# A tap sum and one convolution tap moved between engines in four units of a Hyena-style block (one core)

## The reference, cut to what matters

```
xn    = layernorm(x)
z     = rmsnorm(xn, pre_norm_w) @ in_proj_w.T            # 768 channels
z_pre = causal depthwise conv of z, 3 taps, + short_b
x2, x1, v = split(z_pre)                                 # 256 channels each
h     = sum over 16 states of residues * exp(log_poles * t)
xv    = x1 * v
y     = (longconv(xv, h) + xv * D_skip) * x2
...   # out projection, gated MLP, layernorm, residual, then a second FFN with layernorm
```

## Time and profile before

| | |
|---|---|
| three runs | 1079.39, 1080.0, 1081.58 us; median 1080.0 |
| profiled execution | 1079.64 us, span 1077.8 us |
| busy over the span | PE 98%, DVE 82%, ACT 66%, POOL 28% |
| phase A | to about 189 us of the span |
| phase B | to about 250 us |

### The profile page before, as it was taken

How to read it: one execution, slowest core, us unless ns; L and a number is a source line. 1 busy time by engine, 2 the same in 40 slices (tenths; PEclk the granted TensorE clock), 3 DMA queues, 4 the chain that set the end, 5 groups by cost and what they waited for, 6 DMA issues and landing times.

```text
span 1077.8 us, 24963 instructions
## 1 busy us (share of the span) xinstructions
PE 1054.1 (98%) x9012; PEld 1008.1 (94%) x9012; DVE 880.8 (82%) x2321; ACT 710.9 (66%) x1589; POOL 299.3 (28%) x575
## 2 busy tenths in 40 slices
PE   8899999999999999999999999999999999999998
PEld 7777788889989999999999999989999999999997
DVE  7999998784788788888888778897878888887876
ACT  7878887774465666666666666666656666666644
POOL 6677775460111111211111111121111111111111
PEclk9999999999999999999999999999999999999999
DMA  3337987976533333333333333443333333333000
GB/s 129 119 124 234 296 216 193 378 293 125 108 59 50 50 54 57 50 51 52 55 59 63 60 50 54 119 102 43 53 58 50 51 53 54 58 64 58 22 21 31
DMA packets 112491, 102.83 MB, mean 95 GB/s; under 512 B 7552, under 2 KB 103744, under 8 KB 112112
## 3 DMA queue, kind: packets, MB, share of 16 engines
q1 hardware_dynamic: 111136, 98.67, 41.7%
q0 software_dynamic: 736, 2.51, 0.7%
q10 hardware_dynamic: 496, 0.05, 0.0%
HBM read 75.75 MB, written 30.70 MB: 99 GB/s over the span
## 4 chain that ended last, share of the span: by engine, by line
PE 67%; DVE 7%; issue 2%; ACT 1%; POOL 0%; POOLq 0%; DVEq 0%; ACTq 0%
PE ps_ring L1539 35%; PE ps_w L1539 15%; PE ps_m L1539 9%; PE ps_o L1539 4%; PE ps_rt L1554 2%; DVE base L1361 1%; PE ps_w L1549 1%; DVE bn L1265 1%; PE ps_m L1605 1%; DVE ht_l L1277 1%; DVE prod L1308 0%; DVE pt_l L1277 0%; POOL sc L1117 0%; ACT rows L1242 0%; ACT hid L1203 0%
## 5 line engine op out<-in xcount | busy, mean ns | idle before, releaser
L1117 POOL TENSOR_TENSOR sc<-sc,neg_half 128x2 f32<-128x2 f32 x127 | 94.8, 746 | 677.1 <-DVE sc L1489 405.9
L1182 ACT ACTIVATE gate<-ps_ring 128x256 f32<-128x256 f32 x192 | 72.9, 381 | 125.9 <-PE ps_ring L1539 124.8
L1203 ACT ACTIVATE hid<-ps_ring,b1s 128x256 f32<-128x256 f32 x256 | 112.1, 483 | 27.6 <-PE ps_w L1539 13.3
L1539 PE MATMUL ps_ring<-mt_l,wl_h 128*128 128x256 f32 x640 | 125.8, 278 | 2.6 <-DVE mt_l L1277 2.6
L1539 PE MATMUL ps_ring<-mt_h,wl_h 128*128 128x256 f32 x640 | 125.8, 278 | 1.8 <-DVE prod L1308 1.3
L1539 PE MATMUL ps_ring<-mt_h,wl_l 128*128 128x256 f32 x640 | 125.3, 277 | 0.0
L1277 DVE TENSOR_TENSOR ht_l<-hid,ht_h 128x256 fp32r<-128x256 f32 x256 | 103.2, 423 | 16.6 <-ACT ht_h L1207 10.7
L1539 PE MATMUL ps_ring<-xt_h,we_h 128*128 128x256 f32 x512 | 103.5, 283 | 2.5 <-DVE prod L1308 2.4
L1308 DVE TENSOR_TENSOR prod<-ps_ring,gate 128x256 f32<-128x256 f32 x192 | 80.8, 421 | 24.7 <-ACT gate L1182 21.0
L1539 PE MATMUL ps_ring<-xt_h,we_l 128*128 128x256 f32 x512 | 100.3, 277 | 0.0
L1539 PE MATMUL ps_ring<-xt_l,we_h 128*128 128x256 f32 x512 | 100.3, 277 | 0.0
(11 more groups left out here) (203 smaller groups left out, 2737.1 us busy)
## 6 DMA issues: line engine op xcount, KB each, us to landing
toep_scratch<-taps_scratch SPq DMA_DIRECT2D x26, 512.0 KB, 7.4
toep<-toep_scratch SPq DMA_DIRECT2D x26, 512.0 KB, 7.1
xa<-in_x SPq DMA_DIRECT2D x16, 512.0 KB, 5.1
x_scratch<-x2c SPq DMA_DIRECT2D x16, 512.0 KB, 3.7
x2s<-x_scratch SPq DMA_DIRECT2D x32, 256.0 KB, 6.9
xa_c<-in_x SPq DMA_DIRECT2D x32, 256.0 KB, 2.6
xb_c<-in_x SPq DMA_DIRECT2D x32, 256.0 KB, 2.7
yin<-seq SPq DMA_DIRECT2D x124, 64.0 KB, 6.4
```

Of the source, the lines that this page charges most:

```text
L1117: nc.gpsimd.tensor_tensor(sc[:, to], sc[:, to], neg_half[:, 0, 0:CC], ALU.pow).then_inc(S[done], 1)
L1182: nc.scalar.activation(gate[rows_of, m % 2], ring[m % RING][rows_of, 0], ACT.Gelu_apprx_tanh).then_inc(S["gate_done"], 1)
L1203: nc.scalar.activation(hid[:, m % HIDS], block_of, ACT.Gelu, bias=b1s[:, m:m + 1]).then_inc(S["hid_done"], 1)
L1539: mm = nc.tensor.matmul(out, lhs(a, kk), rhs(b, kk), start=(j == 0), stop=(closed and j == len(todo) - 1))
```

## The change

In the first four units (`u <= LAST_POWERS`, which is 3):

- the sixth block's last tap is made by ScalarE into a second half of `x2_tap` and added by GpSimd, as the fifth's already is, and VectorE's third tap of that block is gone;
- VectorE's second pair of tap sums, which stood behind the fourth block, stands behind the sixth.

In all units `x2_tap` has two halves, and the ring `pole_pow` has 12 tiles in place of 16, which leaves the memory taken as it was. The waits on `x2_done` and `tap_extra` count two additions for each of these units. From unit 4 on the order of the work is the old one.

```diff
-    POWERS = 16
+    POWERS = 12
...
-        x2_tap = sb(ctx, "x2_tap", [P, TA])
+        x2_tap = sb(ctx, "x2_tap", [P, KB, TA])
...
+        def beside(u):
+            return (4, 5) if u <= LAST_POWERS else (4,)
+        def beside_until(u):
+            return sum(len(beside(n)) for n in range(u))
...
-                sp.wait_ge(S["x2_done"], u + 1)
+                sp.wait_ge(S["x2_done"], beside_until(u + 1))
...
-                    pool.wait_ge(S["conv_done"], ZB * n + 5)
-                    pool.wait_ge(S["tap_extra"], n + 1)
-                    nc.gpsimd.tensor_tensor(sums_of(0, n, 2), sums_of(0, n, 2), x2_tap[:], ALU.add
-                                            ).then_inc(S["x2_done"], 1)
+                    for k, i in enumerate(beside(n)):
+                        pool.wait_ge(S["conv_done"], ZB * n + i + 1)
+                        pool.wait_ge(S["tap_extra"], beside_until(n) + k + 1)
+                        nc.gpsimd.tensor_tensor(sums_of(k, n, 2), sums_of(k, n, 2), x2_tap[:, k], ALU.add
+                                                ).then_inc(S["x2_done"], 1)
...
-                if i == 4:
-                    wait(act, S["x2_done"], u)
-                    nc.scalar.activation(x2_tap[:], slot(b)[:], ACT.Copy, scale=sw[:, m, 2:3]
+                if i in beside(u):
+                    wait(act, S["x2_done"], beside_until(u))
+                    nc.scalar.activation(x2_tap[:, m], slot(b)[:], ACT.Copy, scale=sw[:, m, 2:3]
...
-                        if i == 4:
-                            dve.wait_ge(S["tap_extra"], n + 1)
-                        add_tap(n, i, 1, "conv_done" if i == 4 else "mid_done")
+                        if i in beside(n):
+                            dve.wait_ge(S["tap_extra"], beside_until(n) + i - 3)
+                        add_tap(n, i, 1, "conv_done" if i in beside(n) else "mid_done")
...
-                    if valid(n, UA) and i != 4:
+                    if valid(n, UA) and i not in beside(n):
...
-                    if i in (0, 3):
+                    if i in (0, ZB - 1):
                         long_taps(powers_at(n, i))
```

More of the change, by code:

```diff
@@ L358, in carry_x2 @@
             def carry_x2(u):
-                pool.wait_ge(S["x2_done"], u + 1)
+                pool.wait_ge(S["x2_done"], beside_until(u + 1))
                 pool.wait_ge(S["conv_done"], ZB * (u + 1))
@@ L545, in _ @@
                         measure(n + 3, i // 2 if i < 3 else i - 2)
-                    if valid(n, UA) and i != 4:
-                        dve.wait_ge(S["mid_done"], (ZB - 1) * n + (i if i < 4 else 4) + 1)
+                    if valid(n, UA) and i not in beside(n):
+                        dve.wait_ge(S["mid_done"], ZB * n - beside_until(n) + (i if i < 4 else 4) + 1)
                         add_tap(n, i, 2, "conv_done")
-                    if i in (0, 3):
+                    if i in (0, ZB - 1):
                         long_taps(powers_at(n, i))
```

## The result

The changed kernel takes **1082.89 us** (median of 10 runs, 1081.71 to 1084.65) against 1080.1 us for the kernel before (10 runs, 1079.27 to 1081.58). The ratio is 1.0024, 95% interval 1.0016 to 1.0033: 2.8 us slower by the medians. The profiled execution took 1082.88 us, its span is 1081.1 us.

The account below looks back on a forecast made before the run. VectorE bounded units 0 to 3; after the change, loops through ScalarE, GpSimd and VectorE would. Z4 comes 2.8 us late and nothing is caught up: 1080.0 median becomes 1082.8 us (chance 0.58), range 1081.0 to 1084.2.

Parts of the forecast that it names:

- The loop through ScalarE and GpSimd: Units 0 to 3: added copy and second addition precede the row scales, 12.11 us per unit against 11.83; alone Z4 1.9 late.
- The sign of a wrong direction: The prediction called itself wrong in direction if `row_scales` started earlier after Z than 8.0 us.
- The loop with VectorE in it: Moved pair held until GpSimd's second addition ends; VectorE goes on 1.62 us after that addition's start; Z4 2.8 us late.
- The size at Z4: Start of unit 4: Z4 forecast at 72.85 against 70.09 before, phase A 2.8 us late.
- the rival without a hold: New addition does not hold the moved pair; loop through ScalarE and GpSimd decides, +1.9 us, 1081.9; chance 0.22.
- The Trainium skill: Two-SBUF-input VectorE instructions and SBUF-reading GpSimd instructions contend, the second waiting for the first's end; by it the sum is 2.8 us.
- The other side: Rival: idle ScalarE and GpSimd take the work in, units 0 to 3 fall to 10.24 us, 5.0 us faster, 1075.0; chance 0.06.
- The costs put at nothing: The ring of 12 tiles and the sync queue's store of x2 were both claimed to cost nothing.
- the ring: `pole_pow` at 12 tiles: exponentials wait for sum k - 12, already done in time, so no cost.
- The store of x2: Sync queue: it waits for the second addition, with only a store and a load three units ahead behind it; no cost.
- Whether it comes back: After unit 4: units run at 10.24 us with TensorE busy throughout, so nothing of the loss is caught up.

Follow-up runs that it names:

- experiment 3: Changed kernel with the moved pair of tap sums behind the next unit's first block, ahead of that block's own pair: 1082.69 us, ratio 1.0022.
- experiment 5: Changed kernel with GpSimd's second addition behind the next unit's first product and x2 carry, waits asking only for the additions needed: 1082.49 us, ratio 1.0016.
- experiment 2: Changed kernel with the second pair of tap sums put back behind the fourth block, leaving the moved tap alone: 1082.44 us, ratio 1.0017.
- experiment 7: Kernel before with only the ring pole_pow cut from 16 tiles to 12: 1080.28 us, ratio 0.9995.
- experiment 8: Changed kernel run once more, unaltered, for a second profile: 1082.84 us.
- experiment 9: Kernel before with the second pair of tap sums behind the next unit's first block and the sixth block's last tap left on VectorE: 1078.45 us, ratio 0.9979.
- experiment 4: Changed kernel with GpSimd's second addition behind the next unit's row scales and first product, ahead of the x2 carry: 1083.98 us, ratio 1.0031.

## Why the prediction was right, point by point

The forecast of 1082.8 us met the median of 1082.89. Its mechanism held, one term of its sum was too long, and the sum met the median by chance.

- *The loop through ScalarE and GpSimd* was given as 12.11 us per unit and the reason for the loss. Experiment 3 shows it by itself in units 1 and 2, with no pair held: 11.92. In the changed kernel a unit takes 12.03. That the second addition ahead of the row scales is the cause is shown by experiment 5, which takes it out from there and brings the units from those 11.92 to 11.44 with ScalarE's work unchanged and no pair held in either; and experiment 2 shows that the tap without the pair brings the loss. In the prediction's terms: the row scales were to start at Z + 8.03 and start at Z1 + 7.78 (43.60), mainly because the second addition takes 1.09 us and not 1.28; against that the row scales to Z took 4.25, not 4.08.
- *The sign of a wrong direction* was met, and the direction was right. It was to be a start of the row scales earlier than Z + 8.0; they start 7.87, 7.78, 7.78 and 7.75 us after Z. The sign was drawn too close to the sum: with 4.08 us behind it, only a start before 7.75 would have made a unit shorter than the 11.83 of before.
- *The loop with VectorE in it* held in its mechanism, and its one wrong term is the length of the second addition. VectorE starts its units at 31.95, 43.98 and 56.01, 12.03 us apart, where the sum had 12.19. To the product it takes 7.80 us, as forecast (43.98 to 51.78), to the first addition 1.50 more. The pair is held until the second addition ends, and VectorE goes on 0.34 us later (0.33 forecast); but from the addition's start that is 1.43 us (30.52 to 31.95) and not 1.62, because the addition takes 1.09. In units 1 and 2 this loop and the other one end together: VectorE's addition of the sixth block ends at 42.47 and GpSimd is done with its first addition at 42.55. In unit 3 this one alone decides. GpSimd has no idle time between the product and the row scales there, and VectorE's addition of the sixth block was done at 65.95, 0.6 us before the second addition could start:

```profile
63.81 1.30 POOL L384 TENSOR_TENSOR xv<-conv 128x512 f32<-128x512 f32 x1 [1.92 <-DVE conv L513]
...
65.32 2.35 POOL L392 TENSOR_TENSOR x2c<-x2c,x_tap 128x512 f32<-128x512 f32 x2
67.63 0.20 POOL L331 TENSOR_TENSOR apart<-stats 128x4 f32<-128x4 f32 x1
```

- *The size at Z4* was forecast 2.76 us late and is 2.01. The way to Z4 passes the second addition four times, and 4 x 0.19 = 0.76 us is the whole of the difference. The measured 2.01 lies near the 1.9 of the rival without a hold, but not for that rival's reason, since the pair was held (1.33 us in units 0, 1 and 2). What the hold costs can only be estimated: with units 0 to 2 of experiment 3 (11.99, 11.92, 11.92) and unit 3 of experiment 2 (11.31) Z0 to Z4 would be 47.14 us, so the hold is worth about 0.9 of the 2.01, as the prediction had it, and the first loop alone about 1.1, not 1.9. No kernel ran that shows this sum as one.
- *The rest of the 2.8 us* is not in my sum. Of the profile's 2.8 us at the start of phase C (249.69 - 24.09 = 225.60 to 252.07 - 23.70 = 228.37), 0.24 came in Z4 to Z13 and 0.52 after it. Experiments 7 and 8 show that a second profile moves the first by 0.19 and the second by 0.76, so they aren't shown to be the change's. The two spans differ by 3.3 us: phase C took 0.9 us more in the changed kernel's profile (829.0 against 828.1; 829.6 in experiment 8 and 828.7 in experiment 7), and its Z0 came 0.39 us sooner. The interval of the ratio, 1.7 to 3.6 us, holds both 2.0 and 2.8. That the forecast met the median to 0.1 us is chance: its sum was 0.75 us too long at Z4, and in the profile about as much (0.76 us) came behind Z4 that the sum did not have.
- *The Trainium skill* (SBUF — State Buffer, "Who interferes with whom"), by which the second of two such instructions waits for the first's end: the trace agrees for the 512-wide additions, 0.34 us from the end of the addition to VectorE's next start, with the pair's own work in it. It differs for the 8-wide power of 1.67 us: the pair beside it stayed at 0.60 after the change too (33.59, the power from 33.78 to 35.46), and there the measurement stands.
- *The other side* (idle engines take it in) is refuted by the windows: ScalarE and GpSimd are idle for 1.7 and 2.9 us of the 12.03 and the unit is longer all the same.
- *The costs put at nothing*: the ring is confirmed (experiment 7). The store of x2 was harmless in the changed kernel, but experiment 5 shows that this hung on when the addition comes: there it starts 6.6 us later (unit 0's at Z0 + 13.4, in the changed kernel at Z0 + 6.8), and the load behind the store cost 3 us.
- *Whether it comes back*: it did not. Unit 5 took 10.30 us and the stretches from Z4 on are no shorter than before.

## What to carry to other kernels

An engine's idle time says nothing of what another instruction on it costs; close the loop from the instruction back to itself through every engine that it passes, and compare the loop with the time of one round. Before moving work off a saturated engine, look for the instruction on it that takes longer than its likes: here a tap sum of 1383 ns among ones of 346 was worth 1.7 us over four units (experiment 9) for nothing but another place in the order. Where two edits come together, time them apart, and mind what an edit meant to take one thing away puts back elsewhere (experiments 3 and 4).

## What the runs showed of the hardware that was not expected

- GpSimd's second addition takes 1.09 to 1.10 us and the first, with the same shapes, 1.29, wherever the two stand as rows of their own, also where the second stands apart behind the next product (38.20 in experiment 4) and no pair is near. Why was not tried.
- The row scales, eleven small GpSimd instructions, take 4.08 us from start to ScalarE's next chunk in the kernel before, 4.13 in experiment 3 (44.27 to 48.40), 4.25 in the changed kernel, where they start while a pair of tap sums is ending, 4.29 in experiment 4 and 4.37 in experiment 5 (42.67 to 47.04), where a pair runs beside them too. Tenths of this kind, several per unit, are the limit of a sum made from rows.
